# A mixture-of-experts layer on one core: the last batch's router exponential goes to GpSimd, the SiLU table load and one shared FFN unit go ahead of the block loop

## The reference, cut to what matters

```python
shared = silu(x @ shared_gate.T) * (x @ shared_up.T) @ shared_down.T
logits = x @ router_w.T + routing_bias
probs  = sigmoid(logits)
scores, indices = top_k(probs, 2)
scores = scores / sum(scores)
# per token: sum over its 2 experts of score * down(silu(gate(x)) * up(x))
out = x + tanh(g_ffn) * (shared + combined)
```

## Time and profile before

| what | value |
|---|---|
| time, median of 3 runs | 177.18 us (177.13 to 180.12) |
| the profiled execution's own time | 177.18 us |
| its span in the trace | 175.4 us |
| PE, DVE, ACT, POOL busy | 92%, 75%, 64%, 63% of the span |
| attention ends, routing and the first blocks begin | about 107 to 127 us of the span |
| block loop | about 127 to 162 us |
| units 2 and 3, down projection, adding, storing | about 162 to 175 us |

### The profile page before, as it was taken

One profiled execution on the slowest core, in us unless ns is written; L12 is line 12 of the kernel. 1 busy time (PEld: TensorE's weight loads), 2 busy tenths in 40 slices (PEclk: granted clock), 3 DMA queues, 4 the chain that ended last, 5 costly groups with the idle time before them and its releaser, 6 DMA issues.

```text
span 175.4 us, 4620 instructions
## 1 busy us (share of the span) xinstructions
PE 160.6 (92%) x1415; PEld 140.1 (80%) x1415; DVE 131.4 (75%) x621; ACT 111.5 (64%) x427; POOL 110.0 (63%) x139
## 2 busy tenths in 40 slices
PE   7999889999997999999999999996699999999960
PEld 7887669997987998998998988884378788887860
DVE  2879988675999687898697999867794667776283
ACT  4566997775858873958873959732655666665400
POOL 3775799854868554588524687787156456666611
PEclk9999999999999999999999999999999999999998
DMA  5899996730000000000000000013124222211172
GB/s 158 263 374 351 415 396 266 294 124 0 19 2 0 19 2 4 15 32 27 24 4 0 15 21 17 15 50 85 38 65 114 67 67 77 58 51 41 55 241 90
DMA packets 11096, 17.35 MB, mean 99 GB/s; under 512 B 2075, under 2 KB 6945, under 8 KB 10944
## 3 DMA queue, kind: packets, MB, share of 16 engines
q1 hardware_dynamic: 9504, 14.59, 24.6%
q0 software_dynamic: 1280, 2.20, 3.8%
q10 hardware_dynamic: 288, 0.26, 0.4%
HBM read 9.99 MB, written 7.51 MB: 100 GB/s over the span
## 4 chain that ended last, share of the span: by engine, by line
PE 56%; POOL 11%; DVE 9%; issue 9%; ACT 9%; DMA 3%; SPq 1%; DVEq 0%; POOLq 0%
PE o_bank L406 7%; PE misc L417 6%; PE s_even L380 6%; POOL ys L1472 6%; PE pt L391 6%; ACT probs L726 5%; PE proj_q L337 3%; PE proj_k L337 3%; PE misc L487 3%; PE proj_q L338 3%; PE proj_q L339 3%; PE proj_k L339 3%; PE proj_k L338 2%; DMA probs<-ys 2%; PE pt L662 2%
## 5 line engine op out<-in xcount | busy, mean ns | idle before, releaser
L726 ACT ACTIVATE probs<-probs,negmax 128x128 f32<-128x128 f32 x128 | 49.8, 393 | 19.2 <-DVE negmax L951 19.1
L1362 POOL TENSOR_TENSOR probs<-probs,rinv 128x512 f32<-128x512 f32 x32 | 32.9, 1042 | 19.5 <-DVE rinv L965 19.2
L1472 POOL DMA_INDIRECT ys<-probsT,places x23 | 22.5, 979 | 14.7 <-ACT places L866 12.1
L726 ACT ACTIVATION_READ_ACCUMULATOR probs<-probs,negmax 128x1 f32 x128 | 24.3, 190 | 0.0
L1392 POOL DMA_INDIRECT xs<-xrow,slot x16 | 16.3, 1016 | 8.8 <-DVE slot L1065 4.9
L951 DVE CUSTOM_DVE_ANT_0 probs<-s_even,mask 128x128 f32<-128x128 f32 x64 | 18.1, 282 | 3.4 <-issue 3.2
L391 PE MATMUL pt<-ident_sb,probs 128*128 128x128 f32 x128 | 17.9, 278 | 1.9 <-POOL probs L1362 1.3
L380 PE MATMUL s_even<-kT,qT 64*128 64x128 f32 x128 | 18.4, 284 | 0.3 <-DVE negmax L951 0.3
L380 PE MATMUL s_odd<-kT,qT 64*128 64x128 f32 x128 | 18.5, 285 | 0.0
L380 PEld LDWEIGHTS s_even<-kT,qT 64*128 64x128 f32 x128 | 15.4, 187 | 3.5 <-issue 1.2
L951 DVE CUSTOM_DVE_ANT_0 probs<-s_odd,mask 128x128 f32<-128x128 f32 x64 | 18.1, 283 | 0.0
(11 more groups left out here) (282 smaller groups left out, 461.4 us busy)
## 6 DMA issues: line engine op xcount, KB each, us to landing
xs<-pad SPq DMA_DIRECT2D x5, 858.0 KB, 6.9
xg<-xs SPq DMA_DIRECT2D x23, 66.0 KB, 1.9
down_sb<-down SPq DMA_DIRECT2D x1, 1152.0 KB, 10.2
probs<-ys SPq DMA_DIRECT2D x4, 256.0 KB, 4.1
gu_raw<-gu SPq DMA_DIRECT2D x3, 256.0 KB, 5.8
wk_raw<-wkT SPq DMA_DIRECT2D x2, 256.0 KB, 3.6
wq_raw<-wqT SPq DMA_DIRECT2D x2, 256.0 KB, 4.7
mask<-mask SPq DMA_DIRECT2D x8, 64.0 KB, 2.3
```

Of the source, the lines that this page charges most:

```text
L726: e = act.activation(probs[:, r, l, :], probs[:, r, l, :], ACT.Exp, bias=negmax[:, r, l:l + 1], scale=-1.0, accum_out=rowsum[:, r, l:l + 1])
L1362: pool.tensor_tensor(quad, quad, rinv[:, r, 4 * u:4 * u + 4].unsqueeze(2).to_broadcast([P, 4, P]), ALU.mult).then_inc(norm_done, 1)
L1472: pool.indirect_dma_start(out=ys, out_offset=bass.IndirectOffsetOnAxis(ap=places[:, n:n + 1].bitcast(U32), axis=0), in_=y_sb[n % IN_FLIGHT ...
```

## The change

Five edits.

1. **The last exponential.** For r = 4 ACT only copies the 8 logit columns from PSUM to SBUF (`copy_logits`), and POOL computes exp(-logit) as (1/e) to the power of the logit (`power_exp`, 128x8), behind the two counts and the first of the two scatters of batch 6.
2. **The SiLU table** is loaded behind round 3's exponential.
3. **Shared units 0 and 1.** With the table there, `silu(0)` follows at once, and `silu(1)` follows the copy of the logits; `hidden(0)` stands in round 3's choice on DVE, `hidden(1)` in round 4's. Unit 1's passes leave the loop and stand around `x2_transposes(LAST)` on PE, ahead of `ranks(3)`, which was ahead of it.
4. **Attention's tail.** `out_project(6)` goes behind `ranks(2)` on PE, and the copy that it needs, `copy_o(13, 1)`, behind round 2's choice on DVE. On POOL `rstd_second(7)` goes ahead of `count_chosen(2)`.
5. **In the loop over p**, for p = 0 alone, the last step of the odd batch's layer norm (`xrow`, L997) leaves `mask_max(6, ...)` and stands behind `copy_o(4, 0)`.

```diff
@@ PE, tail
             transposes(14, 2)
-            out_project(B - 2, use)
             pe.wait_ge(ez_ready, 3)
             ranks(2)
+            out_project(B - 2, use)
             transposes(15, 3)
@@ PE, behind shared unit 0
             shared_pass(0, 1)
+            pe.wait_ge(table_ready, 1)
+            experts = {n: block_expert(n) for n in range(2)}
+            stay_warm(7)
+            pe.wait_ge(h_done, 1)
+            shared_pass(1, 0)
+            x2_transposes(LAST)
+            shared_pass(1, 1)
             pe.wait_ge(ez_ready, 4)
             ranks(3)
-            pe.wait_ge(table_ready, 1)
-            experts = {n: block_expert(n) for n in range(2)}
-            x2_transposes(LAST)
-            stay_warm(1)
             logits(LAST)
-            stay_warm(5)
@@ PE, block loop
-                if n + 2 == STARTS[UNIT_AT]:
-                    pe.wait_ge(h_done, 1)
-                    shared_pass(1, 0)
-                    shared_pass(1, 1)
@@ ACT
             route_exp(3)
+            act.activation(act_scratch[:], warm[:, 0:1], ACT.Silu)
+            silu(0)
             x2_split(LAST)
-            route_exp(LAST)
-            act.activation(act_scratch[:], warm[:, 0:1], ACT.Silu)
+            copy_logits(LAST)
+            silu(1)
@@ DVE, loop over p
-                mask_max(g + 6, p + 1, 2, after(4, run, steps, 1))
+                mask_max(g + 6, p + 1, 2, after(4, run, steps, 1) if p else iter(()))
                 recips(g + 6, 2, (0,))
                 copy_o(g + 4, 0)
+                finish(steps)
@@ DVE, tail
-            copy_o(13, 1)
             choice = choose_steps(2)
             run(choice, 2)
             recips(15, 3, (0,))
             finish(choice)
+            copy_o(13, 1)
@@ DVE, rounds 3 and 4
             choice = choose_steps(3)
-            run(choice, 3)
+            run(choice, 4)
+            hidden(0)
+            run(norm, 1)
             finish(choice)
+            finish(norm)
             finish(weight_steps(3))
-            run(norm, 1)
             place(3)
-            finish(norm)
...
             choice = choose_steps(LAST)
-            run(choice, 3)
+            run(choice, 2)
             block_lo(0)
             finish(choice)
+            hidden(1)
             finish(weight_steps(LAST))
@@ POOL
+            def power_exp(r):
+                pool.wait_ge(logits_ready, 1)
+                pool.wait_ge(hot_ready, r)
+                pool.wait_ge(inverse_ready, 1)
+                tiles = len(ROUTED[r])
+                pool.tensor_tensor(ez[:, 0:tiles, :].rearrange("p t e -> p (t e)"), inverse_e[:, 0:E_ROUTED * tiles],
+                                   last_logits[:, 0:E_ROUTED * tiles], ALU.pow).then_inc(ez_ready, 1)
...
             scatter(2, 1, 4)
+            rstd_second(B - 1)
             count_chosen(2)
-            rstd_second(B - 1)
             count_chosen(3)
-            scatter(3)
+            scatter(3, 0, 1)
+            power_exp(LAST)
+            scatter(3, 1, 2)
             scatter(LAST)
```

More of the change, by code:

```diff
@@ L44 @@
 HUGE = 3.0e38
+INVERSE_E = 0.36787944117144233
 PROJ_USES = 6
@@ L54 @@
 WARM_UP = 10
-UNIT_AT = 2
 QUOTA_AT = 10
@@ L125, in build @@
         x2_raw = [sb(f"x2_raw{i}", [P, 2, P]) for i in range(2)]
+        inverse_e, last_logits = sb("inverse_e", [P, E_ROUTED]), sb("last_logits", [P, E_ROUTED])
         ez, den, prob = (sb(n, [P, 2, E_ROUTED]) for n in ("ez", "den", "prob"))
@@ L207, in build @@
         half_counted = sem("half_counted")
-        none_ready = sem("none_ready")
+        none_ready, inverse_ready = sem("none_ready"), sem("inverse_ready")
+        logits_ready = sem("logits_ready")
         lg_done, ez_ready = sem("lg_done"), sem("ez_ready")
@@ L761, in x2_split, with copy_logits @@
                 x2_hi(r)
+            def copy_logits(r):
+                act.wait_ge(lg_done, r + 1)
+                act.copy(last_logits[:], route_bank[r][:, 384:384 + E_ROUTED * len(ROUTED[r])]).then_inc(logits_ready, 1)
             def route_exp(r):
@@ L887, in _ @@
                     block_y(n - 1)
[L888 to L891, removed]
             block_y(BLOCKS - 1)
@@ L1293, in _ @@
                     block_lo(n + 2)
-                if n == 1:
-                    hidden(0)
                 run(last_table, 1)
@@ L1299, in _ @@
                 run(last_table, 1)
-                if n + 1 == STARTS[UNIT_AT]:
-                    hidden(1)
                 if n == QUOTA_AT:
@@ L1402, in fills @@
                 pool.memset(none[:], 0.0).then_inc(none_ready, 1)
+                pool.memset(inverse_e[:], INVERSE_E).then_inc(inverse_ready, 1)
                 pool.memset(ones_bf[:], 1.0).then_inc(const_ready, 1)
```

## The result

The changed kernel takes 181.13 us (median of 4, 180.85 to 182.25) against 177.84 for the kernel before, measured beside it (median of 4); the ratio is 1.021, with a 95% interval from 1.013 to 1.029: slower, clear of the noise. The prediction was 177.6, with a range up to 180.2. The profiled execution took 181.39 us, its span is 179.6, 4.2 more than before.

A forecast was written before the change was run, and what follows sets the result against it. PE bounds the block loop; ahead of it the chain ran over the router (table load, then DVE). Norm step -0.6, later loop start +3.4 (attention's tail 0.45 in it), loop -2.4: +0.4 on 177.18 gives 177.6 us, range 175.6 to 180.2.

The forecast's parts named there:

- a hot of over 1 us: Slow-side sign in the changed profile: round 2's hot, in attention's tail, taking over 1 us.
- a granted clock under 1 behind 126: Slow-side sign in the changed profile: PE's granted clock below 1 after 126 us.
- Edit 5, -0.6: Layer norm step at p = 0: moving it removes PE's idle 0.79 us; gain 0 to 0.79, taken -0.6.
- Edit 4, +0.45: Attention's tail: out_project(6) and the last transposes come later, 0 to 1.1 us, taken +0.45 for unit 0.
- rival 2: Attention's tail: round 2's hot still meets POOL's multiply, PE 1.1 us later, 178.7; chance 0.13 shared with another rival.
- Rival 3: PE's clock falls in a 3.5 us gap before the loop; two slow blocks 180.6 us, three 182.0; chance 0.1.
- Edits 1 to 3, +2.95: From unit 0's end to the first block_hidden: this stretch gets longer by 2.95 us.
- the power's 1.68: POOL's power of 128x8 ahead of the loop takes 1.68 us, bounds 0.57 and 1.83.
- The table load: ACT's load of 1.28 us ahead of silu(0) is hidden behind PE's work, ending near 118.4.
- The loop, -2.4: Block loop: without unit 1's passes, silu and hidden it gives back 2.4 us, at least 1.4.
- hidden(0)'s delay: Early loop: hidden(0) delayed the second and third block by 0 to 0.68 us; 0.3 taken as gain.

The follow-up runs named there:

- after_no_meet: The changed kernel with POOL's two multiplies of group 15 cut to one column per head, output not the reference's; 178.21 us, ratio to before 1.002.
- before_units: The kernel before with edits 1 to 3 alone; 178.61 us, ratio to before 1.000.
- after_no_tail: The changed kernel with edit 4 taken back, all else as changed; 177.48 us, ratio to before 0.996.
- before_norm: The kernel before with edit 5 alone; 178.46 us, ratio to before 0.998.
- join: The changed kernel without edit 4, reordered: last experts chosen from logits, POOL raising two, unit 1 following unit 0, round 2's hot earlier; 176.23 us, ratio 0.984.
- power_first: The changed kernel without edit 4, PE's gap filled by nine zero matmuls, the power ahead of both scatters of batch 6; 176.07 us, ratio 0.987.

## Why the prediction was wrong, point by point

The sum was +0.4 and the two spans differ by 4.2. Of the 3.8 us between them 2.44 are edit 4's, 0.97 lie ahead of it, 0.33 in the loop and 0.06 between. Both signs that the prediction named on the slow side came: a hot of over 1 us, and a granted clock under 1 behind 126.

- **Edit 5, -0.6**: right; 0.71 between the two values on PE. The changed kernel's profiled execution started about 1 us late (0.37 + 0.71), in a stretch that is the same in both kernels: PE waited 0.75 us for the first context tile (6.44), and its first matmuls of 256 columns then followed each other every 0.21 us up to 10.3 instead of every 0.12 from about 7; why is open, the granted clock of that stretch being 1.00 in both. Whether the other three executions of the changed kernel started late too, no trace shows. In the nine other kernels with edit 5 that same mask_max(15) had its last read at 106.7 to 107.4, so the 108.00 is of that execution.
- **Edit 4, +0.45**: the step that failed, twice; it cost 2.89. First the overlap of DVE and POOL. The prediction took the choice 0.2 sooner, and it came 0.20 sooner; but it took a hot that begins ahead of POOL's multiply as clear of it, though by its own figures hot ended at 109.65 and the multiply began at 109.62. Hot was caught all the same, ended where it ended before (3.11 behind mask_max(15)), and the copy and out_project(6) now stood behind it. That is rival 2, priced there at 1.1 more; hot's meeting cost 1.1 (after_no_meet), and the order by itself 0.2 where 0.45 were forecast. The copy, where it stood, also kept den clear of the multiply of group 14; den's meeting held the reciprocal behind it up by at most 0.10, and whether hot would have been clear without it no run tests. Second the clock, which the sum put at nothing here: PE has nothing between the transposes of group 14 and ranks(2), and with out_project(6) moved out of that place it idled 1.69 us and paid 1.59 in clock. Rival 3 named the right mechanism, at the other gap, and took from one fall, 4.2 us behind the last matmul, that a shorter gap speaks against one; the runs showed falls behind gaps of 1.69 and 3.77.
- **Edits 1 to 3, +2.95 without edit 4's share**: right to 0.06, and the power's 1.68 to the digit; the power ended 6.96 behind unit 0 (forecast 6.78), and DVE's stretch from block_lo(0) to block_hidden(0) took 3.66 (3.75), so part of the 0.06 is two small misses that cancel. The table load at 119.92 took 1.28, and silu(0) ran at 122.12, right behind unit 0's last pass: the load was hidden, as costed. The Trainium skill's figure ("ScalarE: Activation LUTs", section "What ACT_TABLE_LOAD costs"), 2.66 us for a switch, would by an estimate have held silu(0) until 122.58 (119.92 + 2.66); the trace disagrees.
- **The loop, -2.4**: 0.33 too much; 2.07 in the changed kernel, 2.08 in before_units. The part put on hidden(0)'s delay was the estimate in it.
- **The baseline.** The sum was made against an execution at a clock of 0.997. Most executions of before do not have it. The gap rows of before showed PE's idle times; what they cost in other executions no single trace shows.

Without edit 4 the sum would have been 177.1, and after_no_tail took 177.48; that the forecast fits there so well is in part luck, since its executions lie at clocks of 0.97 to 0.985 and not at the 0.997 that the sum was made for.

## What to carry to other kernels

Before moving an instruction out of the place where an engine waits, ask what that place was covering: out_project(6) was not in the way of ranks(2), it filled PE's wait and kept its clock, and copy_o(13) kept the next DVE step away from POOL. Where a dependent chain leaves PE for some microseconds ahead of a PE-bound stretch, matmuls in the gap are worth a try, useful ones or not: nine zero ones took before to 0.995 and seven took the changed kernel from 181.13 to 179.41, though fourteen took nothing off after_no_tail. A baseline should be timed with its granted clock beside it. A step that begins just ahead of another engine's is not yet clear of it. When a stall from a meeting of two engines is removed, look which instruction runs there next.

## What the runs showed of the hardware

- PE's clock went to its lower level (0.50, 1.2 GHz) behind much shorter gaps than the 4.2 us without a matmul that the trace of before had shown: behind 1.69 us of idle time and 0.70 us of work in 2 us (changed kernel, 112), behind 0.42 us of work in 2 (before_norm, 120), behind 3.77 us idle (changed kernel, 130). The same queue kept its clock in some executions and lost it in others (before: 21 and 60 of 81). When it had fallen it stayed low for 3 to 10 us, in which PE was nearly always busy (9.23 of 10 us in before_norm).
- DVE beside POOL's multiply of 512 columns: den and hot (changed kernel) and total (join) each ended within 0.06 us of the multiply, whatever their size (0.84, 1.27 and 0.85 us where 0.16, 0.19 and 0.12 are usual), hot although it began 0.16 ahead of it. A copy from PSUM of 512 columns beside such a multiply took its usual 0.69, and the reciprocals too (0.12 to 0.18). The Trainium skill, "GPSIMD Engine Reference", section 8 "Key points", speaks of contention with VectorE instructions in a 2-port performance mode or with two SBUF inputs. Hot and total have two, which agrees; den has one and met it all the same, and whether it ran in such a mode no run here shows.
- The power costs by column: 0.72 us for two (join), 1.64 and 1.68 for eight (power_first, changed kernel).
